# A router stage behind a 32-head convolution: half of its sums and two of its norms moved into the convolution, and the contraction walked in another order

## Time and profile before

| what | value |
|---|---|
| median of three runs | 1084.57 us |
| profiled execution, its own time | 1087.74 us |
| its span, first to last instruction | 1085.9 us |
| PE busy | 1046.4 us, 96% of the span |
| DVE busy | 600.7 us, 55% |
| ACT busy | 448.7 us, 41% |
| POOL busy | 612.4 us, 56% |
| mean granted clock of PE | 0.987 of full speed |

### The profile page before, as it was taken

How to read it: one execution, slowest core, us unless ns; L and a number is a source line. 1 busy time by engine, 2 the same in 40 slices (tenths; PEclk the granted TensorE clock), 3 DMA queues, 4 the chain that set the end, 5 groups by cost and what they waited for, 6 DMA issues and landing times.

```text
span 1085.9 us, 13170 instructions
## 1 busy us (share of the span) xinstructions
PE 1046.4 (96%) x4867; PEld 845.7 (78%) x4867; DVE 600.7 (55%) x1041; ACT 448.7 (41%) x798; POOL 612.4 (56%) x452
## 2 busy tenths in 40 slices
PE   6999997899999999999999999999999999999998
PEld 4777775665689988876788888888888888888886
DVE  7999999848865644783622533325333253242224
ACT  5656443821575547554323323223322233322232
POOL 5878994210224562211266776667766667767662
PEclk9999998989999999999999999999999999999999
DMA  8512120000020020033222222533225332232211
GB/s 289 173 49 69 52 56 10 1 1 0 1 79 1 1 70 1 1 141 127 85 91 92 73 73 73 170 139 122 73 73 170 114 129 90 73 112 92 82 65 39
DMA packets 24543, 85.48 MB, mean 79 GB/s; under 512 B 3152, under 2 KB 4832, under 8 KB 23712
## 3 DMA queue, kind: packets, MB, share of 16 engines
q1 hardware_dynamic: 22432, 81.24, 22.0%
q10 hardware_dynamic: 2048, 3.41, 0.9%
HBM read 74.86 MB, written 9.78 MB: 78 GB/s over the span
## 4 chain that ended last, share of the span: by engine, by line
PE 63%; DVE 1%; POOL 1%; issue 1%; ACT 0%; POOLq 0%
PE banks L318 20%; PE banks L320 20%; PE banks L319 20%; PE banks L313 1%; PE banks L1427 1%; POOL wgl L635 0%; DVE stat L1690 0%; PE banks L1436 0%; POOL gul L661 0%; DVE xres L2071 0%; POOL xtr L618 0%; ACT xn L773 0%; DVE xf L1958 0%; PE banks L1492 0%; DVE hf L2082 0%
## 5 line engine op out<-in xcount | busy, mean ns | idle before, releaser
L2082 DVE TENSOR_TENSOR hf<-banks,silu 128x512 f32<-128x512 f32 x132 | 91.3, 692 | 323.9 <-PE banks L320 322.6
L661 POOL TENSOR_TENSOR gul<-wst,guh 128x1280 fp32r<-128x1280 f32 x44 | 129.9, 2952 | 141.7 <-DVE guh L1965 135.8
L671 POOL TENSOR_TENSOR hl<-hf,hh 128x512 fp32r<-128x512 f32 x129 | 178.0, 1409 | 8.9 <-ACT hh L1049 8.9
L1049 ACT ACTIVATE hh<-hf 128x512 fp32r<-128x512 f32 x132 | 83.6, 633 | 190.3 <-DVE hf L2082 190.3
L1085 PE MATMUL banks<-kv,strip 128*128 128x288 f32 x640 | 157.3, 406 | 1.2 <-DVE pr L1665 1.2
L1047 ACT ACTIVATE silu<-banks 128x512 f32<-128x512 f32 x132 | 78.9, 598 | 167.5 <-PE banks L320 167.4
L1085 PEld LDWEIGHTS banks<-kv,strip 128*128 128x128 f32 x640 | 120.7, 190 | 34.0 <-issue 1.6
L318 PE MATMUL banks<-xf,guh 128*128 128x512 f32 x352 | 137.2, 390 | 0.9 <-POOL gul L661 0.9
L319 PE MATMUL banks<-xf,guh 128*128 128x512 f32 x352 | 136.9, 389 | 0.0
L320 PE MATMUL banks<-xf,gul 128*128 128x512 f32 x352 | 136.9, 389 | 0.0
L595 POOL TENSOR_TENSOR rstd<-vare,mhalf 128x2 f32<-128x2 f32 x32 | 25.5, 796 | 165.7 <-DVE vare L1699 165.7
(11 more groups left out here) (289 smaller groups left out, 2238.9 us busy)
## 6 DMA issues: line engine op xcount, KB each, us to landing
wst<-in_chunk_w SPq DMA_DIRECT2D x44, 960.0 KB, 4.7
strip<-toep SPq DMA_DIRECT2D x29, 256.0 KB, 3.0
xf_s<-xf SPq DMA_DIRECT2D x2, 2048.0 KB, 6.8
out<-xres SPq DMA_DIRECT2D x16, 256.0 KB, 2.1
xf<-xf_s SPq DMA_DIRECT2D x8, 512.0 KB, 5.8
mk<-hot_s SPq DMA_DIRECT2D x14, 256.0 KB
xres<-in_x ACTq DMA_DIRECT2D x4, 512.0 KB, 7.1
xres<-in_x SPq DMA_DIRECT2D x2, 1024.0 KB, 5.7
```

The costliest lines, as they stand in the source:

```text
L661: pool.tensor_tensor(gul[:, u, :], wst[:, u, 0:GU_W], f(guh[:, u, :]), ALU.subtract).then_inc(gul_ready, 1)
L671: pool.tensor_tensor(hl[:, u, s, :], hf[:, s, :], f(hh[:, u, s, :]), ALU.subtract)\
L1049: act.activation(hh[:, u, s, :], hf[:, s, :], ACT.Copy).then_inc(hh_ready, 1)
L2082: dve.tensor_tensor(hf[:, s, :], banks[:, 7, :], silu[:, s % 2, :], ALU.mult).then_inc(mul_done, 1)
```

## The change

Four things:

1. **Sums of even tiles.** The eight places whose tile is even (EARLY = 0, 1, 2, 3, 8, 9, 12, 13) are turned by PE at the start of the heads 18 to 25 and added by DVE behind contract(h - 2); the bank is bank 3 of the head's set, and PE waits for the sum before the last four products of the head. The other eight come behind the convolution (SUM_ORDER is the new order of all 16).
2. **Norms of pairs 0 and 1.** DVE's statistics stand behind contract(24) to contract(27), POOL's roots behind the heads 27 and 29, ACT's `apply` behind the heads 28 and 30. The first four `turn_x` stand ahead of END_CONV in PE's queue, two of them in the banks 2 and 3. contract(31) follows contract(30) directly.
3. **The walk of the contraction.** L1663 and L558 keep their places in `pr` but walk the diagonals innermost: DVE writes four words in a row, then skips four, and reads PSUM in steps of 8 words; POOL writes three words in a row, reads `yx` in steps of 10 words and `qx` backwards.
4. **Low parts.** ACT makes five low parts (0, 2, 4, 8, 12) instead of seven, DVE eleven instead of nine. The first four expert products stand in one piece at n = 1 on PE instead of one to two in the rounds 1 to 3.

```diff
+        EARLY = tuple(i for i in range(TILES) if LOG_ORDER[i] % 2 == 0)
+        SUM_ORDER = EARLY + tuple(i for i in range(TILES) if i not in EARLY)
+        SUM_HEAD, PAIR_HEAD = HEADS // 2 + 2, HEADS // 2 + 8
-        LOW_ACT = tuple(range(0, TILES - 2, 2))
+        LOW_ACT = (0, 2, 4, 8, 12)
+        def O_BANK(i):
+            n = SUM_ORDER.index(i)
+            return 4 * ((SUM_HEAD + n) % 2) + 3 if i in EARLY else n % 2
+        def N_BANK(i):
+            return 2 + i if i < 2 else 4 + i % 3
...
 (POOL, opposite)
-                pool.tensor_tensor(view(pr, u, 5, [[HD * HD, MB], [1, 3], [HD, HD]]),
-                                   view(yx, u, WRAP - 1, [[YP_, MB], [HD + WRAP - 1, 3], [1, HD]]),
-                                   view(qx, u, HD - 1, [[2 * HD, MB], [-1, 3], [1, HD]]), ALU.mult)\
+                pool.tensor_tensor(view(pr, u, 5, [[HD * HD, MB], [HD, HD], [1, 3]]),
+                                   view(yx, u, WRAP - 1, [[YP_, MB], [1, HD], [HD + WRAP - 1, 3]]),
+                                   view(qx, u, HD - 1, [[2 * HD, MB], [1, HD], [-1, 3]]), ALU.mult)\
...
 (POOL, the loop over the heads)
+                if h in (PAIR_HEAD + 3, PAIR_HEAD + 5):
+                    pair_root((h - PAIR_HEAD - 3) // 2)
...
 (ACT, the loop over the heads)
+                if h in (PAIR_HEAD + 4, PAIR_HEAD + 6):
+                    apply((h - PAIR_HEAD - 4) // 2)
...
+            after(act, END_CONV)
             for n in range(TILES // 2):
-                apply(n)
-                if n == 0:
-                    after(act, END_CONV)
+                if n > 1:
+                    apply(n)
...
 (PE, the loop over the heads)
+                if even:
+                    pe.wait_ge(conv_out, HEADS // 2)
+                    turn_o(EARLY[h - SUM_HEAD])
                 conv(h, (0, 1, 2))
+                if even:
+                    summed(pe, EARLY[h - SUM_HEAD])
...
 (PE, behind the convolution)
             for i in range(4):
-                turn_o(i)
-            for n in range(TILES // 2):
-                if n + 2 < TILES // 2:
-                    turn_o(2 * n + 4)
-                    turn_o(2 * n + 5)
-                turn_x(2 * n)
-                turn_x(2 * n + 1)
+                turn_x(i)
+            after(pe, END_CONV)
+            turn_o(4)
+            turn_o(5)
+            leave_low(0)
+            pe.wait_ge(pick_set, 3)
+            pe.wait_ge(wB_ready, 2 + KB)
+            for n in range(1, TILES // 2):
+                if n in (1, 3, 5):
+                    for i in SUM_ORDER[TILES // 2 + n + 1:TILES // 2 + n + 3]:
+                        summed(pe, SUM_ORDER[SUM_ORDER.index(i) - 2])
+                        turn_o(i)
+                if n > 1:
+                    turn_x(2 * n)
+                    turn_x(2 * n + 1)
...
 (DVE, contract)
-                rows = y[:, :, 0:4 * HD].rearrange("p m (d i) -> p m d i", d=4)
+                rows = y[:, :, 0:4 * HD].rearrange("p m (d i) -> p m i d", d=4)
...
-                dve.tensor_tensor(view(pr, u, 0, [[HD * HD, MB], [1, 4], [HD, HD]]), rows,
-                                  view(qx, u, 0, [[2 * HD, MB], [1, 4], [1, HD]]), ALU.mult)
+                dve.tensor_tensor(view(pr, u, 0, [[HD * HD, MB], [HD, HD], [1, 4]]), rows,
+                                  view(qx, u, 0, [[2 * HD, MB], [1, HD], [1, 4]]), ALU.mult)
...
 (DVE, the loop over the heads and the router's loop)
-            for h in range(HEADS - 1):
+            for h in range(HEADS):
                 contract(h)
...
-            add_conv(0)
-            add_conv(1)
-            pair(0)
-            contract(HEADS - 1)
+                if SUM_HEAD <= h + 2 < SUM_HEAD + EVENS:
+                    add_conv(EARLY[h + 2 - SUM_HEAD])
+                if PAIR_HEAD <= h < PAIR_HEAD + 4:
+                    n, j = divmod(h - PAIR_HEAD, 2)
+                    pair(n, (j,))
             after(dve, END_CONV)
-            for n in range(TILES // 2):
-                if n > 0:
+            for n in range(1, TILES // 2):
+                if n > 1:
                     pair(n)
-                if n < TILES // 2 - 1:
-                    add_conv(2 * n + 2)
-                    add_conv(2 * n + 3)
-                if n > 0:
-                    low(2 * n - 2)
-                    low(2 * n - 1)
+                if n in (1, 2, 4, 6):
+                    for i in SUM_ORDER[TILES // 2 + (0, 2, 4, 6)[(1, 2, 4, 6).index(n)]:][:2]:
+                        add_conv(i)
+                if n > 1:
+                    low(2 * n - 4)
+                    low(2 * n - 3)
+            low(TILES - 4)
+            low(TILES - 3)
             low(TILES - 2)
             low(TILES - 1)
```

More of the change, by code:

```diff
@@ L602, in low @@
                                    by_eighth(f(cch[:, q % 2, :])), ALU.subtract).then_inc(ccl_ready, 1)
-            for n in range(TILES // 2):
+            for n in range(2, TILES // 2):
                 pair_root(n)
@@ L735, in spread, with tile_of, apply @@
                                rows[:, :, 1:4, HD - WRAP:HD], ACT.Copy).then_inc(y_copied, 1)
+            def tile_of(i):
+                return LOG_ORDER[i] if i < TILES else i % TILES
+            def apply(n):
+                act.wait_ge(pair_rstd, n + 1)
+                for i in (2 * n, 2 * n + 1):
+                    j = i % GROUP
+                    if i >= GROUP:
+                        act.wait_ge(xn_turned, i - GROUP + 1)
+                    rows = ret if 2 * TILES <= i < 3 * TILES else xres
+                    act.activation(xn[:, j, :], rows[:, tile_of(i), :], ACT.Identity,
+                                   bias=nmr[:, j:j + 1], scale=rstd[:, j:j + 1]).then_inc(xn_ready, 1)
             for i in range(4):
@@ L782, in low @@
                     act.wait_ge(xl_left, sum(p <= i for p in LOW_ACT))
-                    act.activation(turned(xtl, tile_of(i)), split(banks[:, 4 + i % 3, :]), ACT.Copy).then_inc(xtl_act, 1)
+                    act.activation(turned(xtl, tile_of(i)), split(banks[:, N_BANK(i), :]), ACT.Copy).then_inc(xtl_act, 1)
             def logits_out(g):
@@ L1089, in conv, with turn_o @@
                     mm.then_inc(conv_done, 1)
+            def turn_o(i):
+                turn(pe, O_BANK(i), turned(qt, LOG_ORDER[i]), o_turned)
             for i in range(GROUP):
@@ L1147, in leave_low @@
                     pe.wait_ge(xth_ready, i + 1)
-                    pe.matmul(split(banks[:, 4 + i % 3, :]), minus[:, :], turned(xth, LOG_ORDER[i]), start=False, stop=True,
+                    pe.matmul(split(banks[:, N_BANK(i), :]), minus[:, :], turned(xth, LOG_ORDER[i]), start=False, stop=True,
                               skip_group_check=True).then_inc(xl_left, 1)
@@ L1210, in _ @@
                 leave_low(2 * n)
[L1211 to L1212 removed]
+                if n == 1:
+                    expert_parts(KB)
                 if n in (4, 5):
@@ L1673, in add_conv, with pair @@
             def add_conv(i):
-                dve.wait_ge(o_turned, i + 1)
+                dve.wait_ge(o_turned, SUM_ORDER.index(i) + 1)
                 t = LOG_ORDER[i]
-                dve.tensor_tensor(xres[:, t, :], xres[:, t, :], banks[:, i % 2, :], ALU.add).then_inc(x_summed, 1)
-            def pair(n):
+                dve.tensor_tensor(xres[:, t, :], xres[:, t, :], banks[:, O_BANK(i), :], ALU.add).then_inc(x_summed, 1)
+            def pair(n, part=range(2)):
                 s = 2 * (n % 2)
@@ L1682, in pair @@
                     dve.wait_ge(xn_ready, 2 * n - 2)
-                for j in range(2):
-                    if n < TILES:
+                for j in part:
+                    if n < TILES // 2:
+                        summed(dve, 2 * n + j)
+                    elif n < TILES:
                         dve.wait_ge(x_summed, 2 * n + j + 1)
@@ L1690, in pair @@
                     i = dve.bn_stats(stat6[:, s + j, :], rows[:, tile, :])
+                if 1 not in part:
+                    return
                 i.then_inc(pair_stats, 1)
```

58 lines of the change are left out of this document (17 added, 41 removed).

## The result

The change made the kernel slightly slower. Its median is 1087.8 us (1083.34 to 1091.53) against 1084.65 us (1082.69 to 1088.6) of the kernel before, 20 runs of each side by side: a ratio of 1.0022 (95%: 1.0011 to 1.0032). The profiled execution took 1085.05 us, span 1083.2 us, mean granted clock 0.994; that of before had 0.987, so the two spans can't be set against each other. Executions with the same mean clock don't settle the size either. Against the 93 executions of the kernel before that ran beside the experiments, the changed kernel's median is 2.1 us slower at 0.987 (1089.8, 4 runs, against 1087.7, 18 runs) and 2.2 at 0.992 (1086.3, 2 runs, against 1084.1, 32 runs), but 0.2 faster at 0.994 (1085.2 against 1085.4, 7 runs each). The verdict rests on the ratio.

The account below looks back on a forecast made before the run. Three places were taken to set the time: the PE-paced heads, the end of contract(31) and the DVE-paced loop. END_CONV 1.6 us earlier and the loop's 4.8 us gave -6.4: 1084.57 - 6.4 = 1078.2 us, range 1074 to 1092.

Parts of the forecast that it names:

- DVE's walk, 2.04 to 1.25 us: L1663 in each head's contraction: the new walk takes 1.25 us, bounds 1.15 to 2.6; called the least certain term.
- the walk gains nothing: Rival, chance 0.14: stepped PSUM reads on DVE as slow as stepped SBUF writes; contract(31) ends at 192.3, time 1084.8 us.
- Sums, 8 x 0.5 = 4.0 us on PE: Heads 18 to 25: four transposes lengthen each by 0.5 us, the convolution by 4.0 us; waiting for the sum costs nothing.
- I keep 1.87: POOL's L558 in each head: the new walk was taken to last 1.87 us as before, bounds 1.5 to 3.3.
- POOL does not seem to pay for the isolated writes: POOL's L558: its products cost 2.4 ns each, L584's with operands in a row 2.5, so little to win.
- POOL has 0.7 us to spare a head, so it costs from 2.6 us on: POOL's head of 4.1 us against 4.85: L558 costs time from 2.6 us, eats the whole gain from about 2.8.
- 4.3 + 1.2 for single heads over 4.85 with room to catch up: DVE in the heads: 4.3 us a head plus 1.2 of moved work exceeds 4.85 only in single heads, then recovers.
- The early 1.9 us: Heads 3 to 10: DVE's faster walk removes three PE stalls of 0.5 to 0.6 us, about 1.9 us in all.
- The loop, 29.4 to 24.6, -4.8 us: Router's loop from END_CONV to the last transposes: 24.6 us in place of 29.4, ACT now leading; 4.8 us saved.
- The sum: Whole kernel: head 31's copy at 180.1, END_CONV at 185.7 (before 187.3), loop -4.8, tail unchanged; together -6.4 us.
- The slower rival: Chance 0.20: POOL's L558 becomes the bound; about 1085 us at 2.8 us, 1099 at its upper bound of 3.3.
- The forecast's own test: DVE's softmax (L1747) expected near 220.7 us; the forecast is wrong if it starts later than 225 us.

Follow-up runs that it names:

- the fifth kernel: The changed kernel with the old walks on both DVE and POOL, the rest of the change kept: 1087.08 us, 1.0021 of the kernel before.
- the sixth kernel: The kernel before with only the new walks of DVE and POOL added: 1086.78 us, 1.0012 of the kernel before.
- the ninth: The changed kernel with POOL's old walk and the norms of pairs 0 and 1 back behind END_CONV: 1087.78 us, 1.0008 of the kernel before.

## Why the prediction was wrong

- **DVE's walk, 2.04 to 1.25 us: right.** 1.22 us, against 1.15 for 1024 words at the rate of L1669 (2.29 us for 2048): the PSUM operand read in steps of eight words costs 0.07 us at most. Rival "the walk gains nothing" fell, and its numbers described the fifth kernel well, where it is true by construction: end of the convolution 192.3 worked out, 192.71 measured.
- **Sums, 8 x 0.5 = 4.0 us on PE: right.** 8 x 0.44 = 3.5 us (5.29 - 4.85 a head); PE has no wait in these heads, so the sum was never late.
- **"I keep 1.87" for L558: wrong by 0.57 us.** Its bounds (1.5 to 3.3) held 2.43. The step "POOL does not seem to pay for the isolated writes" compared two different instructions; within one, runs with plain reads win 0.17, and stepped and backward reads cost more than that (0.53, 0.21).
- **"POOL has 0.7 us to spare a head, so it costs from 2.6 us on": the step that failed.** At 2.43 us POOL is below that: its head is 154.06 to 158.70 us, 4.64, and plain heads still last 4.85. Yet the old walk brings 6.4 us at the end of the convolution (191.61 to 185.25). I had asked only whether POOL's queue gets longer than PE's head. It acts in three other ways. The longer POOL's line runs, the longer and the likelier a small line of DVE's is held (4.2 us in the heads 25 and 27 and 1.8 in the early ones). A root of the early heads waits behind it, and ACT and PE with the root (1.6). And the reduction waits 0.64 us a head for it (12.8 us in 20), so DVE keeps no reserve, and 0.6 in the last contraction. The 4.1 us of POOL's head also left out what else stands in its queue: L584 in four heads (1.27 us) and the early roots (0.9). In head 24 the former made DVE's reduction of head 25 wait 1.33 us, just ahead of the held lines.
- **"4.3 + 1.2 for single heads over 4.85 with room to catch up": failed with it.** The pairs' two small lines were in a price of 0.55 for all the rest of a pair's norms. In head 25 they took 3.1 us, 159.78 to 162.91, and PE waited 2.96 us for the walk behind them. No later head gives that back: 4.85 us is PE's own pace. Spare time on DVE gives PE nothing back.
- **The early 1.9 us:** 0.26 in the changed kernel (head 10's copy at 75.91 us, before 76.17), for the hold and the roots. With the old POOL walk it is 2.7 (73.44).
- **The loop, 29.4 to 24.6, -4.8 us:** measured up to the softmax, -4.0 (39.8 to 35.8). Forecast were 35.0 (24.6 + 10.4). Among the kernels with all of parts 1, 2 and 4 it lies between 35.7 and 37.2, so the term was too large by 0.7 to 2.2 us; which round loses it wasn't followed.
- **The sum:** by head 31's copy (185.52, before 178.02) the convolution lost 7.5 us: -0.3 early, +3.5 of sums, +4.3 at the two holds. Forecast was +2.1. From that copy to the end of the contraction -3.2 us (forecast -3.7), from there to the softmax -4.0 (-4.8). So of the 6.7 us between 220.7 and 227.4, 5.4 were lost in the heads. The time is 9.6 us over the forecast (1087.8 against 1078.2); the other 2.9 us lie behind the softmax or in how executions differ, which stays open.
- **The slower rival** had the right engine and, for the changed kernel, the wrong mechanism and threshold: POOL as bound of the heads, from 2.6 us. POOL paces heads only in the sixth kernel, and there at 2.43 us already, in those with L584. The forecast's own test (wrong if the softmax starts after 225 us) gave the right verdict: 227.39.

The hold could be read in the trace of before. The minimum, median and maximum of the small line of all pairs were
```profile
L1697 DVE TENSOR_SCALAR vare<-mom x32: 168/169/592, 182.0 to 496.3; 128x2 f32<-128x2 f32 x32
```
and the 592 is the first of them, which ran beside the only long POOL instruction of that part (181.29 to 182.54 us, L588); in the early heads, with POOL at work most of the time, the mean was 725 ns. Behind the convolution POOL is mostly idle, so the line looks free where the earlier trace rows price it. The Trainium skill, SBUF — State Buffer, Who interferes with whom, says that DVE and GpSimd share one pair of ports, which whoever comes first keeps for the whole instruction, and that a tensor_scalar of DVE's can be of the kind that needs it, while a tensor_reduce or a tensor_tensor with one operand in PSUM is not. The trace agrees in each point: 1.36 and 1.94 us for L1723 and L1725, ended by POOL's instructions; L1691 at 2.29 and L1685 at 1.22 us beside POOL; and L1725 at 0.16 us where it came 0.01 us before POOL's L559. It is a rule that would have named the hold, and I did not weigh it.

The other page that was weighed spoke against POOL's walk: by GPSIMD Engine Reference, Performance pitfalls for Q7 kernels, of the Trainium skill, a read step above 8 bytes costs half as much again per element, 2.8 us here (an estimate from it). Measured, yx in steps of ten words makes 2.23 of 1.69 us, 32% more for one of two inputs; the direction held and the size did not.

**What stays open.** The profiled softmax is 0.3 us late, the medians differ by 3.15 us and the ratio says 2.4. The clock has a part in how executions differ: of the 93 of the kernel before that ran beside the experiments, those at 0.987 took 1087.7 us and those at 0.997 took 1082.4 us. It was low more often in the changed kernel, at 0.989 or less in 11 of 20 runs against 26 of 93. That PE's new idle time in the convolution (2.96 and 0.81 us) does this isn't shown, and two kernels speak against it: in the fifth PE waited 0.82, 0.22 and 2.35 us there and no run of 12 was below 0.991, in the ninth it didn't wait there and 6 of 12 were at 0.985 or 0.986. Nor was it tried whether the pairs' small lines could stand on DVE where POOL is idle.

## What to carry over

Before moving small DVE instructions into a stretch where POOL works without a break, look up the same instruction's maximum in the trace, not its median, and see which POOL instruction it ended with: its price there is up to the length of POOL's longest line. "It has 0.7 us to spare" is a statement on an engine's throughput; ask also who waits for its instruction each round, and who is locked out while it runs. The version worth keeping is the fourth: the change with POOL's old walk and the pairs' small lines on ACT, 1077.1 and 1077.7 us in two sets of runs, 0.993 and 0.995 of the kernel before.

## What the runs showed of the hardware

A DVE line of two elements from SBUF to SBUF took 0.17 us with POOL idle and up to 2.22 us (at 22.03 us of the changed kernel) beside it, while walks, reductions and statistics kept their times; ACT's lines for the same values took 0.19 to 0.21 us. A DVE product with a PSUM operand in steps of eight words and an output in runs of four moves 1024 words in 1.22 us. On POOL 768 products took 1.69 us (runs of three written, no steps on the read side), 1.87 (isolated writes, reads in runs of eight), 2.23 (runs of three written, one operand read in steps of ten words) and 2.43 (the other in threes backwards besides).
